# Key spans of 7 nodes placed by a register on PE, in a graph network kernel

## The reference, cut to what matters

```
h = relu(layernorm(x)); x = x + GCN(h)      # 3 convolutions
h = relu(layernorm(x)); x = x + GRU(sum over edges of (h[src] + relvec[rel]), h)
conv(h, W, b) = segment_sum((h @ W)[src] * norm, dst) + b
norm = dinv[src] * dinv[dst],  dinv = 1 / sqrt(degree)     # one more edge of each node to itself
```

## Time and profile before

| | us |
|---|---|
| median of 3 runs | 956.23 |
| the profiled execution | 956.55 |
| its span, first to last instruction | 952.4 |
| preparation, to the verdict | 0 to 20 |
| build with beats | 20 to 97 |
| build with products of convolution 1 | 97 to 330 |
| layers | 330 to 952 |

### The profile page before, as it was taken

How to read it: one execution, slowest core, us unless ns; L and a number is a source line. 1 busy time by engine, 2 the same in 40 slices (tenths; PEclk the granted TensorE clock), 3 DMA queues, 4 the chain that set the end, 5 groups by cost and what they waited for, 6 DMA issues and landing times.

```text
span 952.4 us, 15806 instructions
## 1 busy us (share of the span) xinstructions
PE 912.0 (96%) x6296; PEld 567.6 (60%) x6296; DVE 480.3 (50%) x1267; ACT 284.9 (30%) x556; POOL 28.4 (3%) x41
## 2 busy tenths in 40 slices
PE   2889999999999999999999999999999999999996
PEld 1457888888888884544444544445454455555553
DVE  7966999899999710211112323333534043333436
ACT  3355555555555510111001022211232112112222
POOL 0210100000000000000000000000000000000000
PEclk8779999999999999999999999999999999999999
DMA  6000000000000040000000001111311001000011
GB/s 208 8 1 1 8 12 13 13 13 13 13 13 14 16 158 1 1 1 1 1 0 23 24 28 44 45 41 36 118 46 31 8 22 30 27 23 22 23 34 30
DMA packets 27350, 27.65 MB, mean 29 GB/s; under 512 B 3217, under 2 KB 25901, under 8 KB 27272
## 3 DMA queue, kind: packets, MB, share of 16 engines
q1 hardware_dynamic: 26600, 26.18, 8.7%
q10 hardware_dynamic: 672, 0.41, 0.2%
HBM read 17.43 MB, written 9.15 MB: 28 GB/s over the span
## 4 chain that ended last, share of the span: by engine, by line
PE 92%; DVE 5%; ACT 1%; issue 1%; DMA 0%; SPq 0%; DVEq 0%; ACTq 0%
PE ps L1112 41%; PE ps L805 12%; PE ps L712 11%; PE ps L554 9%; PE ps L1123 5%; PE ps L558 5%; PE ps L1143 2%; PE ps L786 2%; DVE node_b L814 1%; PE ps L717 1%; PE ps L728 1%; PE ps L754 1%; PE ps L774 1%; PE ps L539 1%; DMA count<-in_dst 0%
## 5 line engine op out<-in xcount | busy, mean ns | idle before, releaser
L1112 PE MATMUL ps<-count,node_b 128*128 128x512 f16 (+3 forms) x1400 | 271.2, 351 | 0.4 <-DVE node_b L1274 0.3
L814 DVE TENSOR_TENSOR node_b<-node_b 128x50 f16<-128x50 f16 (+4 forms) x455 | 209.0, 524 | 8.6 <-PE ps L712 7.8
L1112 PEld LDWEIGHTS ps<-count,node_b 128*128 128x128 f16 (+2 forms) x1400 | 121.4, 97 | 142.4 <-issue 8.2
L712 PE MATMUL ps<-node_b 128*128 128x225 f16 (+1 forms) x808 | 165.8, 288 | 10.9 <-DVE node_b L814 10.9
L1025 ACT ACTIVATE count<-ps 128x500 f32 x202 | 122.9, 608 | 124.7 <-PE ps L712 119.7
L805 PE MATMUL ps<-node_a,count 128*128 128x256 f16 (+1 forms) x1050 | 149.1, 273 | 0.0
L1112 PE MATMUL ps<-count,node_a 128*128 128x512 f16 (+3 forms) x700 | 135.4, 352 | 0.0
L805 PEld LDWEIGHTS ps<-node_a,count 128*128 128x128 f16 (+1 forms) x1050 | 99.7, 98 | 21.9 <-issue 8.4
L1112 PEld LDWEIGHTS ps<-count,node_a 128*128 128x128 f16 (+1 forms) x700 | 59.9, 97 | 74.2 <-issue 6.7
L717 PE MATMUL ps<-node_b,params 128*128 128x9 f16 (+1 forms) x808 | 101.5, 174 | 0.0
L712 PEld LDWEIGHTS ps<-node_b 128*128 128x128 f16 x808 | 81.3, 101 | 18.1 <-DVE node_b L814 8.8
(11 more groups left out here) (198 smaller groups left out, 812.1 us busy)
## 6 DMA issues: line engine op xcount, KB each, us to landing
node_a<-in_x SPq DMA_DIRECT2D x4, 768.0 KB, 7.4
table_scratch<-agg SPq DMA_DIRECT2D x21, 128.0 KB, 1.7
node_b<-table_scratch SPq DMA_DIRECT2D x3, 768.0 KB, 6.6
xt<-x_scratch SPq DMA_DIRECT2D x16, 128.0 KB, 2.2
out<-scaled SPq DMA_DIRECT2D x16, 128.0 KB, 1.7
xt<-in_x SPq DMA_DIRECT2D x12, 128.0 KB, 2.0
params<-in_x SPq DMA_DIRECT2D x12, 128.0 KB, 2.1
x_scratch<-xt SPq DMA_DIRECT2D x12, 128.0 KB, 1.7
```

The source lines that it names most:

```text
L712: return PE.matmul(window(s)[:, :, first:first + n], low, key_hot[k][j // 2][:, j % 2, :, i].rearrange("p (t w) -> p t w", w=n), start=(s ...
L814: return DVE.tensor_tensor(to, iota, keys.unsqueeze(2).to_broadcast([P, n, width, 2]), ALU.is_equal)
L1112: last = PE.matmul(ps[:, b, 0:cols], nodes[0:k, t, part, f * P:(f + 1) * P], count[0:k, t, c * CHUNK:c * CHUNK + cols], start=(n == 0 and ...
```

## The change

- `SPANS` is replaced by `SPAN = 7` in all four quarters: each `sources` matmul has 25 x 7 = 175 columns. The span of quarter j starts at the node of the quarter's own first edge, held between 0 and 13 of the 20 columns; quarter 0 starts at 0.
- The three offsets of a super block are computed before the build: ACT's queue loads the first destination of every quarter (805 elements of 4 bytes, and one), POOL subtracts the super block's first and clips.
- `build_pe` loads the offsets into registers with `load_offsets`, 12 for four super blocks (once before the first super block, then behind the windows of super blocks 3, 7, ...), and the `sources` matmuls of quarters 1 to 3 write at an address from a register.
- `relations` works on all 20 columns; DVE makes its one-hot of 20 ranks (`rank_hot`, 320 elements for four super blocks) where it made one of 11.
- `low_k` and `key_k` lie as [quarter, super block]; the key one-hot of a pair is one instruction of 1400 elements.
- Preparation: the rules become four, and the work on `starts` and the iotas stands ahead of the wait for `dst`. ACT computes `rank_r` (two instructions of 512) between the copies, and copies `low_k` out at once.

```diff
-SPANS = ((0, 9), (2, 9), (5, 11), (9, 11))
+SPAN = 7
...
         def prepare_pool():
...
+            POOL.wait_ge(starts_in, 32)
+            POOL.wait_ge(quarters_in, 32)
+            POOL.tensor_tensor(offsets, offsets, starts.unsqueeze(2).to_broadcast([1, NS, QUARTERS]), ALU.subtract).then_inc(offsets_step, 1)
+            POOL.wait_ge(offsets_step, 1)
+            POOL.tensor_scalar(offsets, offsets, float(WINDOW - SPAN), 0.0, ALU.min, ALU.max).then_inc(offsets_step, 1)
...
         def prepare_act():
...
             ACTE.wait_ge(pads_set, PADS)
+            by_quarters = offsets.rearrange("p s j -> p (s j)")
+            ACTE.dma_start(by_quarters[:, 0:E // P], dst[0:E // P * P].rearrange("(p s e) -> p s e", p=1, e=P)[:, :, 0],
+                           allow_slow_non_contiguous=True).then_inc(quarters_in, 16)
...
             ACTE.activation(low_r, low_row, ACT.Copy).then_inc(rows_cast, 1)
+            turned_out(0, low_k)
+            ACTE.wait_ge(firsts_negated, 1)
+            for q in range(Q):
+                ACTE.activation(rank_r[:, q, :], dst_row[:, q, :], ACT.Identity, bias=neg_first[:, q:q + 1]).then_inc(rows_cast, 1)
             ACTE.wait_ge(types_in, 64)
             ACTE.activation(rel_r, rel_row, ACT.Copy).then_inc(rows_cast, 1)
...
+        def load_offsets(s):
+            n = min(LOADS, NS - s)
+            return nc.values_load_multi_w_load_instructions(
+                offsets[:, s:s + n, 1:QUARTERS], engines=[mybir.EngineType.PE], min_val=0, max_val=WINDOW - SPAN,
+                skip_runtime_bounds_check_because="every offset was cut to 0 and WINDOW - SPAN")[1]
...
         def build_pe():
             PE.wait_ge(keys_out, 5)
             PE.wait_ge(rel_cleared_wide, 2)
+            PE.wait_ge(offsets_step, 2 + QUARTERS - LAST_FULL)
...
-                for j, (first, n) in enumerate(SPANS):
+                if s == 0:
+                    offset_of = load_offsets(s)
+                for j in range(QUARTERS):
                     low = low_hot[k][:, j, :, i]
+                    first = bass.ds(offset_of[s % LOADS * (QUARTERS - 1) + j - 1], SPAN) if j else slice(0, SPAN)
...
-                        return PE.matmul(window(s)[:, :, first:first + n], low,
-                                         key_hot[k][j // 2][:, j % 2, :, i].rearrange("p (t w) -> p t w", w=n), start=(s == 0 and j == 0),
-                                         stop=(j == QUARTERS - 1), skip_group_check=True)
+                        return PE.matmul(window(s)[:, :, first], low, key_hot[k][:, j, :, i].rearrange("p (t w) -> p t w", w=SPAN),
+                                         start=(s == 0 and j == 0), stop=(j == QUARTERS - 1), skip_group_check=True)
...
                         sources().then_inc(win_done, 1)
+                if (s + 1) % LOADS == 0 and s + 1 < NS:
+                    offset_of = load_offsets(s + 1)
                 for w in range(BEATS * (s - 1), BEATS * s):
...
         def build_dve():
...
-                one_hot(low_hot[k], low_k[:, m, :, :], 0, P).then_inc(*dve_seq.up())
-                one_hot(key_hot[k][0], key_k[:, m, 0:2, :], 0, T * SPANS[0][1]).then_inc(*dve_seq.up())
+                one_hot(low_hot[k], low_k[:, :, s0:s0 + 2], 0, P).then_inc(*dve_seq.up())
                 one_hot(carry_hot[k].unsqueeze(1), carry_k[:, s0:s0 + 2].unsqueeze(1), 1, T).then_inc(*dve_seq.up())
-                one_hot(key_hot[k][1], key_k[:, m, 2:4, :], 0, T * SPANS[2][1]).then_inc(hot_made, 1)
+                one_hot(key_hot[k], key_k[:, :, s0:s0 + 2], 0, T * SPAN).then_inc(hot_made, 1)
```

More of the change, by code:

```diff
@@ L62, in program @@
     NC = -(-N // CHUNK)
-    IOTA = T * max(n for _, n in SPANS)
-    SPAN = max(n for _, n in SPANS)
+    IOTA = T * SPAN
     LAST_FULL = -(-LEFT // P)
     assert D == 2 * P and FULL == NS - 1 and NS < Q * P and TAIL <= REL_ROW - 11 and R <= 16 and PAIRS * 2 == NS and BATCH == 2
-    assert SPANS[0][0] == 0 and sum(SPANS[-1]) == WINDOW and all(b[0] <= sum(a) for a, b in zip(SPANS, SPANS[1:])) and KEYS <= BANK
-    assert all(SPANS[j][1] == SPANS[j + 1][1] for j in range(0, QUARTERS, 2)) and IOTA > max(P, T, R)
-    assert 2 * LEFT >= LAST_FULL * P
+    assert E % P and KEYS <= BANK and IOTA > max(P, T, R)
+    assert 2 * LEFT >= LAST_FULL * P and LAST_FULL == 2 and QUARTERS == 4 and 2 * SPAN + SPAN - 1 >= WINDOW
     SETTLES = EARLY + EARLY % 2
@@ L121, in program @@
             early(Q * SUPER, I32).rearrange("p (q e) -> p q e", q=Q) for _ in range(5))
-        low_r, key_r, rel_r, span_r = (early(Q * SUPER // 2).bitcast(F16).rearrange("p (q e) -> p q e", q=Q)
-                                       for _ in range(4))
+        low_r, key_r, rel_r, span_r, rank_r = (early(Q * SUPER // 2).bitcast(F16).rearrange("p (q e) -> p q e", q=Q)
+                                       for _ in range(5))
         shared_r, carry_r = (early(Q * P // 2).bitcast(F16).rearrange("p (q e) -> p q e", q=Q) for _ in range(2))
+        RULES = 4
         next_row = early(Q, I32)
@@ L274, in prepare_pool @@
             POOL.iota(steps_w, pattern=[[0, Q], [1, WINDOW]], base=0, channel_multiplier=0).then_inc(iotas_made, 1)
+            POOL.wait_ge(starts_in, 32)
[3 more added lines that the diff above has]
+            POOL.tensor_scalar(offsets, offsets, float(WINDOW - SPAN), 0.0, ALU.min, ALU.max).then_inc(offsets_step, 1)
+            POOL.wait_ge(offsets_step, 2)
+            for j in range(LAST_FULL, QUARTERS):
+                POOL.memset(offsets[:, NS - 1, j:j + 1], min((j - 1) * SPAN, WINDOW - SPAN)).then_inc(offsets_step, 1)
         def prepare_act():
@@ L343, in prepare_dve @@
             DVE.tensor_copy(ident16[:, :], ident[:, :]).then_inc(ident16_made, 1)
[L344 to L361, removed]
-            DVE.wait_ge(rank_and_key, 4)
-            DVE.scalar_tensor_tensor(out=carry_r, in0=high_row[:, :, last], scalar=1.0, in1=shared_r,
-                                     op0=ALU.add, op1=ALU.mult).then_inc(rank_and_key, 1)
             DVE.wait_ge(iotas_made, 1)
@@ L402, in prepare_pe @@
             PE.wait_ge(ident16_made, 1)
-            for bank, (row, ready, n) in enumerate(((low_r, rows_cast, 1), (rel_r, rows_cast, 2), (span_r, rank_and_key, 1),
-                                                    (key_r, rank_and_key, 3), (carry_r, rank_and_key, 5))):
+            for bank, (row, ready, n) in enumerate(((low_r, rows_cast, 1), (rank_r, rows_cast, 1 + Q), (rel_r, rows_cast, 2 + Q),
+                                                    (key_r, span_and_key, 2), (carry_r, span_and_key, 4))):
                 PE.wait_ge(ready, n)
```

111 lines of the change are left out of this document (67 added, 44 removed).

## The result

The changed kernel takes 1035.05 us (median of 4 runs, 1033.29 to 1037.78) against 956.12 us: ratio 1.083, 95% interval 1.080 to 1.086, 79 us slower. The forecast was slower, 1090 us in a range of 1000 to 1180. The profiled execution has a span of 1029.8 us (before 952.4).

A forecast was written before the change was run, and what follows sets the result against it. PE was taken as the bound, by its matmul columns, with DVE close behind. 956.55 us + 129 (45 groups) + 3 (first part of the build) + 1 (preparation) = 1090 us, range 1000 to 1180.

The forecast's parts named there:

- Columns: PE's window matmuls: narrower windows save 0.15 us a block, 0.6 us a group, -27 us over 45 groups.
- Length of the load: PE's load of twelve registers lasts 2.6 us, from 0.21 us a register on ACT; bounds 0.9 to 3.5 us.
- The stock: PE's sequencer leads the array by about two issued matmuls, 0.2 us, read from the wait at L707.
- Exposed in a group: PE idles at the register load, once in each group of four blocks: 2.5 us not hidden.
- Register addresses: Matmuls addressed from a register on PE cost 0.03 us each, 12 a group: +0.36 us a group.
- The clock: Pauses at the loads drop PE's clock to the lower level in part of the groups: +0.6 us a group.
- The group: Four super blocks in the full-clock stretch: +2.86 us each, 8.0 us where there were 5.1.
- First part of the build: Blocks 0 to 19, with five loads: +3 us, between -4 and +13.
- Preparation: Work ahead of the build: verdict earlier, keys later; +1 us, between -1 and +3.
- Half hidden: Rival: products behind the load reach PE's array while it runs, 1.9 us a group exposed; 1035 us, chance 0.18.
- products that start inside a load: Sign in PE's trace that was to show the half hidden rival: products starting while a register load runs.
- The queue of 64 entries: TensorE's instruction queue: if all used, 32 matmuls in stock hide the load; first rival, 927 to 945 us, chance 0.14.

The follow-up runs named there:

- no_register: The changed kernel without register loads and register addresses on PE, key spans at fixed columns 0, 4, 9 and 13: 928.46 us, ratio 0.972.
- short_load: The changed kernel loading 3 registers instead of 12 every fourth block, all four blocks using the first one's offsets: 929.16 us, ratio 0.972.
- packed: The changed kernel with POOL packing a block's three offsets into one integer; PE loads 4 registers a group and unpacks them: 941.93 us, ratio 0.986.
- packed_late: packed with the transfer of the 805 quarter starts issued behind the rel loads instead of ahead of src and rel: 941.88 us.

## Why the prediction was right, and where not

The direction, the place and the mechanism stand: a long load on PE's sequencer, idle time by "issue" behind it, in each group. Point by point:

**Columns: right in kind, 0.5 us a group instead of 0.6.** A block with five products went from 1.19 to 1.05 us (263.06 to 264.11), 0.14 by the starts, but the mean block of no_register is only 0.126 shorter than before's: -22.7 us in the stretch for -27 forecast. That no_register is 27.1 us under before in all, the very number of the forecast, is chance: 6.3 of it were won in the first 20 blocks.

**DVE: right.** It is late for nobody in the stretch (busy 179 of 304 us, 1.99 us a pair where 1.85 was forecast).

**Length of the load: 2.9, not 2.6 us.** The slope of 0.21 came from two loads of ACT; PE's is 0.24. It lay inside the bounds. This alone would have made the forecast worse, 14 us higher.

**The stock: the step that failed.** "PE's stock of issued work is about two matmuls, 0.2 us" became 15 matmuls and 1.0 us. The wait at 200.8 was read as that of the block at 201.11, since 0.3 us is what one expects of a short lead. But the waits recur once a block and look all alike, and it belonged to the block at 202.30. The proof stood in the same row: the last of these waits starts at 328.5, and the last window of the build starts at

```profile
330.02 0.27 PE L712 MATMUL ps<-node_b 128*128 128x225 f16 x1
```

of the kernel before: 1.5 us ahead. In the kernel after, the wait at 262.8 belongs to the window at 264.11, 1.3 us ahead. With the 1.0 us that was left in stock when the loads began and PE's 2.9 us the step would have given 1.9 us a group for 2.5: 0.6 x 45 = 27 us less.

**Exposed in a group: 1.9, not 2.5 us.** That is the measured 90.0 us over 46 loads, less 0.08 each: what the step gives with the right stock.

**Register addresses: nothing, not 0.36 us a group.** short_load shows it, 0.7 us in all. 16 of the 55 us by which the forecast was too high. It is nothing only while the sequencer is faster than the array; packed's six instructions a block are the other case.

**The clock: right in kind, 0.3 us a group instead of 0.6.** It fell to 0.50 nine times after 97 us, for 3.4 us each; one of them and what follows it:

```profile
144.10:147.50 3.40, 3.40 (x26) 2.15 (x23) 0.78 (x2) 1.19 (x2) 0.42 (x1) 0.50 0.02 5
147.50:151.00 3.50, 1.89 (x28) 1.60 (x25) 2.98 (x8) 1.19 (x2) 0.00 (x0) 1.00 0.00 0
```

3.4 us of work at half speed is at most 1.7 us lost, 15 us in all. The stretch's balance, 74.2 = -22.7 (the columns, by no_register) + 84.6 (45 x 1.88) + clock, leaves 12 us for it, within that bound. In 36 of 45 groups the pause is there and the clock stays, so the length of the pause alone does not decide it; what does stays open.

**The group: 6.75, not 8.0 us** (303.9 / 45). Its terms: 5.1 - 0.5 + 1.9 + 0.3; what is left is rounding.

**First part of the build:** +3 forecast, -1.3 measured, within its bounds.

**Preparation:** +1 forecast, +2.8 measured, within its bounds. The issue took 0.8 us, not 1.3 to 4.7 (and 0.9 for the one element more); the price was elsewhere: the packets delayed src, and POOL's passes slowed DVE. The saving set against it did not come, because the line was misread: L301 copies `rel_k` and `span_k`, not the keys. Both copies stayed scattered and took as long after:

```profile
17.19 3.79 ACT L322 ACTIVATE node_b<-ps 128x808 f16<-128x808 f16 x2 [0.18 <-PE ps L432]
```

**The rivals.** "Half hidden" named 1035 us, the time that came, by a mechanism that did not happen: it let 0.6 us of products behind the load pass it. What is hidden is 1.0 us of work ahead of it. The two errors of its sum (its 1.9 us exposed have another reason, and its 0.36 of arithmetic stands where 0.3 of clock was lost) cancel. The prediction's own sign for it, "products that start inside a load", is seen in the trace and would have misled, were program order not compared. The queue of 64 entries (the Trainium skill, "TensorE: Matmul & The Clock Gate", table of specifications) was taken as 32 matmuls. A load started with 15 to 17 matmuls of two instructions each outstanding, 30 to 34: the page was nearer to it than the reading that outvoted it, though only half of its figure was seen.

## What to carry to other kernels

A load of registers on an engine's sequencer is hidden only up to the stock of work issued ahead of it, and only if the sequencer can rebuild that stock before the next: check the load's length against the stock, and the sequencer's sum a block against the array's. Moving or splitting the load helps with the first, only fewer registers and operations with the second; fewer, packed values turned 8% slower into 1.4% faster here, 1.7% with the load behind the products. Before reading a lead from a recurring wait, count the waits from the end, where the last one has only one block it can belong to.

## What was not expected of the hardware

- PE's sequencer executes register loads about 15 matmuls ahead of the array (17 with the load behind products) and waits up to 17 ahead, ACT's at 46.1 only when the instruction before has been handed over the earlier trace rows.
- A load costs 0.24 us a register on PE with no floor to speak of: 0.523, 0.767, 0.992, 1.486 and 2.916 us for 2, 3, 4, 6 and 12. "Runtime: NRT & Kernel Launch" of the Trainium skill (Instruction fetch mechanics) gives some 200 ns a register for a TENSOR_LOAD; these, from on-chip memory, cost a little more.
- An operation of DVE slows down beside POOL's: L359 took 2.04 us while POOL worked at 9.39 (1.79 us), and its twin 0.69 us in packed_late, where POOL was idle then.
